# Sending TensorE's first two pipelined slots through the loop of all later slots, with idle feed-forward products in them, in place of a loop of their own

## The chip, the cores and the metric

The kernel runs on one core of one Trainium2 chip, as one launch. The metric is the device time of that core in microseconds. All engines of the core run their own instruction streams and meet only at semaphores.

## What is computed

The reference is one adaLN block over 8 sequences of 256 tokens and 128 channels. A layer norm, a modulation and an eight-head attention come first (the kernel's first part). Then the result is modulated again and goes through six layers, each a windowed attention with 16 heads and a feed-forward part:

```python
for i in range(DEPTH):                       # DEPTH = 6
    x = attn_layer(shift_tokens(x), Wqkv[i], q_scale[i], k_scale[i], Wo[i]) + x
    x = ffn_layer(shift_tokens(x), ln_g[i], ln_b[i], W1[i], b1[i], W2[i], b2[i]) + x

def ffn_layer(x, g, bln, W1, b1, W2, b2):
    mu = x.mean(-1, keepdims=True)
    var = ((x - mu) ** 2).mean(-1, keepdims=True)
    xn = (x - mu) / jnp.sqrt(var + 1e-05) * g + bln
    a, gate = jnp.split(xn @ W1 + b1, 2, -1)
    return a * jax.nn.gelu(gate, approximate=False) @ W2 + b2
```

## The kernel before

The six layers are run as a pipeline of 48 slots: slot g carries sequence g mod 8 of layer g // 8. In slot g, TensorE (`slot` of its block, L956) does

- the scores of sequence g and the end of the attention of g - 1 (`turn_q`, `turn_k`, `turn_p`, `attend`, `turn_o`, `project_out`);
- the projections of the next sequence (`q`, `k`, `v`, through `project_in`, L740);
- if `norm` is set, the two averages of the feed-forward's layer norm for f = g - 2: `mean` (L897) and `variance` (L901);
- if `ff` is set, the feed-forward products for f = g - 3 (`LAG` is 3): `gates_01`, `gate_2` and `values` (18 matmuls of 256 columns, recorded at L908 to L910) and `down` (L947, recorded at L952).

ScalarE, VectorE and GpSimd have slots of their own with the same meaning of g. SyncE moves v into place by DMA and loads the weights of the next layer. Work is ordered by hand on each engine; every wait is on a count of a semaphore. All counts start from a credit of 8 that VectorE hands out at the start, so that the first sequences wait for nothing that does not exist.

Slots 0 to 2 have no feed-forward work yet. On TensorE slot 0 is written out; slots 1 and 2 are a loop of their own (`pe.Fori(1, LAG)`, without `norm` and `ff`); behind it stand `mean(0, 5)` and `variance(0, 6)`, the layer norm of sequence 0 in banks 5 and 6 of PSUM; then comes the long loop `pe.Fori(LAG, SLOTS - 1)` over slots 3 to 46, and slot 47 is written out. In step with that piece VectorE subtracts the mean of sequence 0 at the end of its slot 2, ScalarE squares and inverts behind its slot 2 (`square`, `inverse_deviation`, `round_norm`), and GpSimd runs `divide`, `scale_norm` and `rest` behind its slot 2, where `split_up` (the low part of W1) has just run. The loops of ScalarE and GpSimd over layers begin at slot 3; VectorE's loop does too.

Of the kernel before, what the change touches and what calls it, by code (L numbers as in the profile page):

```python
# [21 lines left out]
F32 = mybir.dt.float32  # L22
# [29 lines left out]
HP = N + 1  # L52
NEG = -1e30
CREDIT = 8

LAST_BANKS = {SLOTS - 3: (2, 3, 1), SLOTS - 2: (5, 4, 0), SLOTS - 1: (2, 3, 1)}

# [9 lines left out]
def build(nc, xT, w1s, w2s, w3T, woT, cT, wmod, wqkv, scales, wo, params, w1, w2, consts, out):  # L67
    with ExitStack() as ctx:
# [210 lines left out]
        def layer_of(f):  # L279
            return f >> 3  # L280
# [12 lines left out]
        def _(sp):  # L293
# [32 lines left out]
                sp.wait_ge(s["f_prod"], CREDIT + 3 * B * layer)  # L326
                sp.dma_start(par[:, L_BA:L_END], params[layer, :, L_BA:L_END]).then_inc(s["p_h_loaded"], 16)

            def load_down(layer):
                sp.wait_ge(s["f_down"], CREDIT + B * layer)  # L330
                sp.dma_start(w2_sb[:, 0:2, :], w2[layer, 0:256, :].rearrange("(c p) e -> p c e", p=P))\
                  .then_inc(s["w_2_loaded"], 16)
                sp.dma_start(w2_sb[0:HT[2][1], 2, :], w2[layer, 256:HID, :]).then_inc(s["w_2_loaded"], 16)
                sp.wait_ge(s["f_done"], CREDIT + B * layer)
                sp.dma_start(par[:, L_B2:L_BA], params[layer, :, L_B2:L_BA]).then_inc(s["p_o_loaded"], 16)
# [56 lines left out]
            load_out(0)  # L392
            load_norm(0)
            load_hidden(0)
            load_down(0)
            sp.wait_ge(s["zeroed"], 6)
            layer_body(0, True)
            with sp.Fori(1, DEPTH - 1) as layer:
                layer_body(layer, True)
# [8 lines left out]
        def _(pool):  # L408
# [2 lines left out]
            pool.memset(w1_hi[:, :, :].bitcast(F32), 0.0).then_inc(s["zeroed"], 1)  # L411
            pool.memset(w1_lo[:, :, :].bitcast(F32), 0.0).then_inc(s["zeroed"], 1)
            pool.memset(k_t[:, :, :], 0.0).then_inc(s["zeroed"], 1)

            def low(pair, m):

# [45 lines left out]
            def divide(f):  # L462
                pool.wait_ge(s["f_rstd"], CREDIT + f + 1)
                pool.wait_ge(s["f_centred"], CREDIT + f + 1)
                pool.wait_ge(s["f_split"], CREDIT + f)
                pool.tensor_tensor(f_y, f_c, f_r, ALU.mult).then_inc(s["f_normed"], 1)

            def scale_norm(f):
                pool.wait_ge(s["f_normed"], CREDIT + f + 1)
                pool.wait_ge(s["p_n_loaded"], 16 * layer_of(f) + 16)  # L470
                pool.sem_inc(s["pool_waited"], 1)
                pool.tensor_scalar(f_y, f_y, par[:, L_G:L_G + 1], par[:, L_B:L_B + 1],
                                   ALU.mult, ALU.add).then_inc(s["f_scaled"], 1)

            def rest(f):
                pool.wait_ge(s["f_high"], CREDIT + f + 1)
                pool.tensor_tensor(f_lo[:, :], f_y, f_hi[:, :].bitcast(F32), ALU.subtract).then_inc(s["f_split"], 1)

            def slot(g, norm=True, ahead=True, more=True, after=None, layer=None):

                f = g - 2
                scale(g, 1)
                if ahead:
                    rotate(g + 1, 0, 0)
                    low(g + 1, 1)
                    rotate(g + 1, 0, 1)
                    if after == 7:
                        table(layer, 1)
                        split_weights(layer, 2)
                    scale(g + 1, 0)  # L490
                    if after == 6:
                        table(layer, 0)
                if norm:
                    divide(f)
                    scale_norm(f)
                if ahead:
                    rotate(g + 1, 1, 0)
                    if after == 6:
                        split_weights(layer, 0)
                if norm:  # L500
                    rest(f)
                if ahead:
                    if more:
                        low(g + 2, 0)
                    if after == 6:
                        split_weights(layer, 1)
                    rotate(g + 1, 1, 1)
                    if after == 2:
                        split_up(layer)
# [29 lines left out]
            rotate(0, 1, 1)  # L539
            slot(0, norm=False)  # L540
            slot(1, norm=False)
            slot(2, norm=False, after=2, layer=0)
            divide(0)
            scale_norm(0)
            rest(0)
            with pool.Fori(0, DEPTH - 1) as layer:
                first = pool.snap(layer * B)
                with pool.Fori(LAG, 6) as b:
# [17 lines left out]
        def _(pe):  # L566
# [190 lines left out]
            def k_read(n):  # L757
                pe.wait_ge(s["roped"], CREDIT + 4 * n + 4)
                pe.wait_ge(s["squared"], CREDIT + 2 * n + 2)
# [137 lines left out]
            def mean(f, bank):  # L897
                pe.wait_ge(s["f_shifted"], CREDIT + 2 * f + 2)
                pe.matmul(ps[:, bank, 0:N], mean_w, f_x, start=True, stop=True).then_inc(s["f_mean"], 1)

            def variance(f, bank):  # L901
                pe.wait_ge(s["f_squared"], CREDIT + f + 1)
                pe.matmul(ps[:, bank, 0:N], mean_w, f_sq, start=True, stop=True).then_inc(s["f_var"], 1)
# [42 lines left out]

            def down(f, bank=1, gated=f_a):  # L947
                pe.wait_ge(s["f_prod"], CREDIT + 3 * f + 3)
                pe.wait_ge(s["w_2_loaded"], 32 * layer_of(f) + 32)
                for i in range(3):  # L950
                    size = HT[i][1]
                    mm = pe.matmul(ps[:, bank, 0:N], w2_sb[0:size, i, :], gated[0:size, i, :],  # L952
                                   start=(i == 0), stop=(i == 2))
                mm.then_inc(s["f_down"], 1)
# [53 lines left out]
                        q_read(2 * g + 3)  # L1008
                        down(g - LAG)

            pe.wait_ge(s["zeroed"], 6)
            pe.wait_ge(s["bf_ready"], 2)
            q(0, 0)
            pe.wait_ge(s["ln_log"], 2 * NC)
# [3 lines left out]
            q_read(0)  # L1018
            v(0, 0)
            slot(0, att=False, norm=False, ff=False)  # L1020
            with pe.Fori(1, LAG) as g:
                slot(pe.snap(g), norm=False, ff=False)
            mean(0, 5)
            k_read(2 * LAG + 1)
            variance(0, 6)
            with pe.Fori(LAG, SLOTS - 1) as g:
                slot(pe.snap(g))
            g = SLOTS - 1
            slot(g, ahead=False)
# [35 lines left out]
        def _(act):  # L1065
# [152 lines left out]
            def square(f):  # L1218
                act.wait_ge(s["f_centred"], CREDIT + f + 1)
                act.wait_ge(s["f_var"], CREDIT + f)  # L1220
                act.activation(f_sq, f_c, ACT.Square).then_inc(s["f_squared"], 1)
# [8 lines left out]
            def round_norm(f):  # L1230
                act.wait_ge(s["f_scaled"], CREDIT + f + 1)
                act.wait_ge(s["f_value_up"], CREDIT + 2 * f)
                act.activation(f_hi[:, :], f_y, ACT.Copy).then_inc(s["f_high"], 1)
# [77 lines left out]
            ln_square(act, 2, 1)  # L1311
            ln_inverse(act, 1, 1)
            ln_square(act, 3, 1)
            act.wait_ge(s["zeroed"], 6)
            act.wait_ge(s["h0_ready"], 1)
            high(0, 0)
            high(0, 1)
# [10 lines left out]
            act.wait_ge(s["h0_ready"], B)  # L1328
            slot(0, att=False, shifted=False, norm=False, ff=False)
            slot(1, shifted=False, norm=False, ff=False)  # L1330
            slot(2, norm=False, ff=False, after=2, layer=0)
            square(0)
            inverse_deviation(0, 6)
            round_norm(0)
            with act.Fori(0, DEPTH - 1) as layer:
                first = act.snap(layer * B)
                with act.Fori(LAG, 6) as b:
# [30 lines left out]
        @block.vector  # L1368
        def _(dve):
            for name in credited:  # L1370
                dve.sem_inc(s[name], CREDIT)

            dve.memset(norm2[:, :, :], 1e-24).then_inc(s["floored"], 1)
            dve.wait_ge(s["silu_e"], 1)
# [131 lines left out]
            ln_centre(dve, 1, 1)  # L1506
            a_residual(3)
            ln_centre(dve, 2, 1)
            dve.wait_ge(s["zeroed"], 6)
            modulate(0)  # L1510
            ln_centre(dve, 3, 1)

# [82 lines left out]
                dve.scalar_tensor_tensor(of_sequence(h0, f), ps[:, bank, 0:N], par[:, L_B2:L_B2 + 1],  # L1595
                                         of_sequence(h1, f), ALU.add, ALU.add).then_inc(s["f_done"], 1)

            def slot(g, att=True, norm=True, ff=True, ahead=True, first_mean=False):
                if att:
                    normalise(g - 1, 0, 0)  # L1600
                    normalise(g - 1, 0, 1)
                centre(g, 0, 0)
                centre(g, 0, 1)
                if ahead:
                    rope_products(g + 1, 0, 0)
                    rope_products(g + 1, 0, 1)
                if ff:
                    product(g - LAG, 2, ps[:, 2, 0:N], 1)
                if norm:
                    subtract_mean(g - 2)  # L1610
                if ff:
                    product(g - LAG, 0, ps[:, 3, 0:N], 2)
                    product(g - LAG, 1, ps[:, 3, N:2 * N], 2)
                if att:
                    normalise(g - 1, 1, 0)
                if ahead:
                    norms(g + 1, 0)
                if att:
                    normalise(g - 1, 1, 1)

                centre(g, 1, 0)
                centre(g, 1, 1)
                if ahead:
                    rope_products(g + 1, 1, 0)
                    rope_products(g + 1, 1, 1)
                    if att:
                        residual(g - 1)
                    if ff:
                        add(g - LAG)
                    if first_mean:  # L1630
                        subtract_mean(0, 5)
                    norms(g + 1, 1)

            def final(b):
# [16 lines left out]
            dve.memset(h1[:, :].rearrange("p (b t) -> p b t", b=B)[:, :, 0:1], 0.0)  # L1651
            slot(0, att=False, norm=False, ff=False)
            slot(1, norm=False, ff=False)
            slot(2, norm=False, ff=False, first_mean=True)
            with dve.Fori(LAG, SLOTS - 1) as g:
                slot(dve.snap(g))
            g = SLOTS - 1
# [113 lines left out]
```

## Time and profile before

| | |
|---|---|
| three timed runs | 1684.33, 1684.33, 1689.32 us, median 1684.33 |
| profiled execution | 1680.68 us, of which the span from first to last instruction 1678.7 us |
| TensorE matmul busy | 1566.1 us (93% of the span) |
| TensorE weight loads, beside them | 1273.2 us (76%) |
| VectorE busy | 1312.9 us (78%) |
| ScalarE busy | 1279.2 us (76%) |
| GpSimd busy | 1070.6 us (64%) |
| mean granted TensorE clock | 0.974 of full speed |

A share of busy time is an average over the first part, the start of the pipeline, its long even stretch and its end, which have different limits. What a change near the start is worth is read from the stretch around it, and from whether the stretches behind it follow TensorE. In a timeline row, the number in brackets is the time that the engine sat idle just before the row, with what ended it; "issue" means that the profile shows no releaser.

### The profile page before, as it was taken

To read this page: it belongs to the slowest core of one execution; us is meant where nothing else is said; L and a number is where in the kernel's file an instruction comes from. 1 tells how busy PE (TensorE), PEld (TensorE's weight loads), DVE (VectorE), ACT (ScalarE), POOL (GpSimd) and SP (SyncE) were. 2 spreads that over 40 slices of the span, in tenths; PEclk is the share of its full clock that TensorE was granted. 3 is DMA by queue.
4 is the path that set the end of the run, shared out by engine and by line. 5 is a ranking of instruction groups with operands and counts; after the bars stand their busy time and mean duration, and the time that the engine had idled before them with its cause. 6 is when DMAs were issued, how large, how long until landed. Compare 5 with 4: busy or idle time off the path is not lost. (4 is left out here: it accounts for less than half of the span.)

```text
span 1678.7 us, 89801 instructions
## 1 busy us (share of the span) xinstructions
PE 1566.1 (93%) x36892; PEld 1273.2 (76%) x36892; DVE 1312.9 (78%) x1953; ACT 1279.2 (76%) x2006; POOL 1070.6 (64%) x783
## 2 busy tenths in 40 slices
PE   7897588999999999999999999999999999999987
PEld 3565466788887888887888887888878888888866
DVE  5576776878888888887887888878878888888853
ACT  4795456778888788887888878888778788787863
POOL 2202656678776778767769667678676787767731
PEclk9899698999999999999999999999999999999999
DMA  3000233222333223324232343222342223322221
GB/s 126 2 0 1 49 73 90 65 65 62 87 77 101 67 68 73 91 56 110 70 71 64 79 110 76 62 65 64 94 115 52 69 70 73 91 56 69 70 54 47
DMA packets 75732, 116.82 MB, mean 70 GB/s; under 512 B 17294, under 2 KB 27276, under 8 KB 74764
## 3 DMA queue, kind: packets, MB, share of 16 engines
q1 hardware_dynamic: 75660, 115.99, 27.8%
q8 instruction: 29, 0.48, 0.1%
q14 instruction: 43, 0.35, 0.1%
HBM read 19.04 MB, written 1.05 MB: 12 GB/s over the span
## 5 line engine op out<-in xcount | busy, mean ns | idle before, releaser
L430 POOL TENSOR_TENSOR arena<-arena 128x1024 f32<-128x1024 f32 x192 | 456.4, 2377 | 95.3 <-DVE arena L1526 81.5
L439 POOL TENSOR_TENSOR arena<-arena,rnorm 128x1024 f32<-128x1024 f32 x192 | 361.8, 1906 | 218.8 <-ACT rnorm L1163 218.8
L628 PE MATMUL ps<-cst,arena 64*128 64x64 f32 x6656 | 293.7, 231 | 44.7 <-issue 15.1
L628 PEld LDWEIGHTS ps<-cst,arena 64*128 64x128 f32 x6656 | 251.9, 141 | 102.9 <-issue 88.8
L1152 ACT ACTIVATE arena<-ps 128x1024 f32<-128x1024 f32 x192 | 197.1, 1026 | 112.9 <-DVE arena L1526 111.7
L1522 DVE TENSOR_TENSOR arena<-ps,rope 128x1024 f32<-128x1024 f32 x192 | 233.6, 1217 | 34.9 <-PE ps L749 34.8
L1526 DVE TENSOR_TENSOR arena<-ps,rope 128x1024 f32<-128x1024 f32 x192 | 233.1, 1214 | 0.0
L748 PE MATMUL ps<-wqkv_lo,x_hi 128*128 128x512 f32 x576 | 229.0, 397 | 0.0
L749 PE MATMUL ps<-wqkv_hi,x_hi 128*128 128x512 f32 x576 | 228.5, 397 | 0.0
L1536 DVE TENSOR_REDUCE norm<-arena 128x16 f32<-128x1024 f32 x192 | 224.4, 1209 | 0.2 <-ACT arena L1152 0.2
L745 PE MATMUL ps<-wqkv_hi,x_lo 128*128 128x512 f32 x576 | 201.2, 431 | 0.6 <-issue 0.6
L869 PE MATMUL ps<-v_sb,arena 64*32 64x66 f32 x12288 | 167.5, 228 | 12.8 <-DVE h L1595 9.0
L820 PE MATMUL ps<-k_t,arena 64*32 64x64 f32 x12288 | 170.2, 229 | 4.4 <-issue 4.4
L893 PE MATMUL ps<-arena,wo_sb 128*128 128x256 f32 x768 | 173.7, 379 | 0.0
L869 PEld LDWEIGHTS ps<-v_sb,arena 64*32 64x32 f32 x12288 | 136.9, 107 | 40.6 <-issue 33.5
L893 PEld LDWEIGHTS ps<-arena,wo_sb 128*128 128x128 f32 x768 | 145.8, 190 | 20.0
L820 PEld LDWEIGHTS ps<-k_t,arena 64*32 64x32 f32 x12288 | 137.8, 107 | 29.3 <-issue 7.5
L1548 DVE TENSOR_REDUCE rmax<-ps 128x8 f32<-128x512 f32 x192 | 130.7, 681 | 23.9 <-PE ps L820 23.8
L1552 DVE TENSOR_TENSOR arena<-ps,rmax 128x512 f32<-128x512 f32 x192 | 132.7, 691 | 14.4
L1564 DVE TENSOR_TENSOR arena<-ps,rden 128x512 f32<-128x512 f32 x192 | 132.7, 691 | 14.4
L1170 ACT ACTIVATE arena<-ps 128x1024 f32<-128x1024 f32 x96 | 98.5, 1026 | 44.9 <-PE ps L628 32.5
L1208 ACT ACTIVATE arena<-ps 128x1024 f32<-128x1024 f32 x96 | 98.5, 1026 | 41.1 <-PE ps L628 36.7
(122 smaller groups left out, 2715.8 us busy)
## 6 DMA issues: line engine op xcount, KB each, us to landing
v_sb<-v_nat SPq DMA_DIRECT2D x576, 130.0 KB
v_sb<-v_nat SPq DMA_DIRECT2D x192, 65.0 KB
wqkv_sb<-wqkv SPq DMA_DIRECT2D x6, 1536.0 KB, 6.4
v_sb<-v_sb SPq DMA_DIRECT2D x96, 65.0 KB
wo_sb<-wo SPq DMA_DIRECT2D x6, 512.0 KB, 3.9
w_sb<-w SPq DMA_DIRECT2D x6, 341.0 KB, 4.2
x<-xT SPq DMA_DIRECT2D x1, 1024.0 KB, 5.0
scl<-scales SPq DMA_DIRECT2D x6, 128.0 KB, 6.1
```

Of the source, the lines that this page charges most:

```text
L430: pool.tensor_tensor(t_cos[:, m, j, :], t_cos[:, m, j, :], t_sin[:, j, :], ALU.add)\
L439: pool.tensor_tensor(x, x, rnorm[:, H * j:H * j + H].unsqueeze(2).to_broadcast([P, H, D]), ALU.mult).then_inc(s[done], 1)
L628: mm = pe.transpose(ps[0:width, bank + t, 64 * c:64 * c + 64], src[r], ident[r, r], tile_position=(64 * t, 0))
L745: pe.matmul(ps[:, bank + c, :], x_lo[:, m, :], wqkv_hi[:, w], start=True, stop=False)
L748: pe.matmul(ps[:, bank + c, :], x_hi[:, m, :], wqkv_lo[:, w], start=False, stop=False)
L749: mm = pe.matmul(ps[:, bank + c, :], x_hi[:, m, :], wqkv_hi[:, w], start=False, stop=True)
L820: mm = pe.matmul(ps[W * w:W * w + W, bank + c, SPAN * hh:SPAN * hh + SPAN], q_t[r, 4 * g + hh, W * w:W * w + W], k_t[r, 4 * g + hh, P * m ...
L869: mm = pe.matmul(ps[W * w:W * w + W, bank + c, ON * hh:ON * hh + ON], p_t[r, h, W * w:W * w + W], v_sb[r, m, w, VD * h:VD * h + ON], start ...
L893: mm = pe.matmul(ps[:, bank, 0:N], wo_sb[:, c, :], o_t[:, c, :], start=(c == 0), stop=(c == H // 2 - 1), skip_group_check=True)
L1522: dve.tensor_tensor(t_cos[:, m, j, :].rearrange("p (h d) -> p h d", h=H), src.rearrange("p a (h d) -> p (a h) d", h=8), tc.unsqueeze(1).to ...
L1526: dve.tensor_tensor(t_sin[:, j, :].rearrange("p (h s d) -> p h s d", h=H, s=2), src.rearrange("p a (h s d) -> p (a h) s d", h=8, s=2)[:, : ...
L1536: dve.tensor_reduce(norm2[:, H * j:H * j + H, 0], sq[:, j, :].rearrange("p (h d) -> p h d", h=H), AX.X, ALU.add).then_inc(s["normed"], 1)
```

## The change

TensorE's loop over slots 1 and 2, and the mean and variance behind it, are taken out; the long loop starts at slot 1. So slots 1 and 2 now issue the feed-forward products for f = -2 and -1 and slot 1 the averages for f = -1. Nobody reads these results. The credits of the semaphores that they count up are lower by as many counts (`UNREAD`), `f_hi` and `f_lo`, which the products read, are zeroed by two more memsets on GpSimd, W2's semaphore gets a credit because its count is now compared with a number worked out from f + 8, and W2's first load no longer waits. The layer norm of sequence 0 moves into slot 2 of all four engines, where the later sequences have it.

```diff
+UNREAD = {"f_mean": 1, "f_var": 1, "f_gate_up": 4, "f_value_up": 4, "f_down": 2}
+W2_CREDIT = 32
...
-            def load_down(layer):
-                sp.wait_ge(s["f_down"], CREDIT + B * layer)
+            def load_down(layer, later=True):
+                if later:
+                    sp.wait_ge(s["f_down"], CREDIT + B * layer)
...
+            pool.memset(f_hi[:, :].bitcast(F32), 0.0).then_inc(s["zeroed"], 1)
+            pool.memset(f_lo[:, :].bitcast(F32), 0.0).then_inc(s["zeroed"], 1)
...
-            slot(2, norm=False, after=2, layer=0)
-            divide(0)
-            scale_norm(0)
-            rest(0)
+            slot(2, after=2, layer=0)
             with pool.Fori(0, DEPTH - 1) as layer:
...
             def down(f, bank=1, gated=f_a):
                 pe.wait_ge(s["f_prod"], CREDIT + 3 * f + 3)
-                pe.wait_ge(s["w_2_loaded"], 32 * layer_of(f) + 32)
+                pe.wait_ge(s["w_2_loaded"], W2_CREDIT + 32 * layer_of(f + B))
...
             slot(0, att=False, norm=False, ff=False)
-            with pe.Fori(1, LAG) as g:
-                slot(pe.snap(g), norm=False, ff=False)
-            mean(0, 5)
-            k_read(2 * LAG + 1)
-            variance(0, 6)
-            with pe.Fori(LAG, SLOTS - 1) as g:
+            pe.wait_ge(s["w_2_loaded"], W2_CREDIT + 32)
+            with pe.Fori(1, SLOTS - 1) as g:
                 slot(pe.snap(g))
...
             slot(1, shifted=False, norm=False, ff=False)
-            slot(2, norm=False, ff=False, after=2, layer=0)
-            square(0)
-            inverse_deviation(0, 6)
-            round_norm(0)
+            act.wait_ge(s["f_mean"], CREDIT)
+            slot(2, ff=False, after=2, layer=0)
             with act.Fori(0, DEPTH - 1) as layer:
...
             for name in credited:
-                dve.sem_inc(s[name], CREDIT)
+                dve.sem_inc(s[name], CREDIT - UNREAD.get(name, 0))
+            dve.sem_inc(s["w_2_loaded"], W2_CREDIT)
...
-            slot(2, norm=False, ff=False, first_mean=True)
+            slot(2, ff=False)
             with dve.Fori(LAG, SLOTS - 1) as g:
```

The waits for `zeroed` go from 6 to 8 everywhere. The rows below are built instruction rows, in the order in which an engine has them; line numbers of the changed kernel are 3 or 4 higher than before (L748 is the projection's L745, L911 to L913 are L908 to L910). TensorE before, from the end of the loop over slots 1 and 2 into the long loop:

```order
L748 MATMUL ps<-wqkv_lo,x_hi 128x512
L749 MATMUL ps<-wqkv_hi,x_hi 128x512
L1021 REGISTER_ALU
L1021 COMPARE_AND_BRANCH
L899 MATMUL ps<-f_a1,cst 128x256
L903 MATMUL ps<-f_a2,cst 128x256
L1026 UNCONDITIONAL_BRANCH
L1026 ISA
L628 MATMUL ps<-cst,arena 128x64 x16
L848 ISA
```

L899 and L903 are the mean and the variance of sequence 0, the second unconditional branch belongs to the long loop's head, and the last row is `turn_q` of slot 3. TensorE in the changed kernel, from the last projection of slot 0 into the loop:

```order
L751 MATMUL ps<-wqkv_lo,x_hi 128x512
L752 MATMUL ps<-wqkv_hi,x_hi 128x512
L1025 UNCONDITIONAL_BRANCH
L1025 ISA
L631 MATMUL ps<-cst,arena 128x64 x16
L851 ISA
L852 ISA
L757 ISA
```

The one loop is now entered right behind slot 0, and its body is that of the long loop. TensorE in the changed kernel, in the middle of the body, which slots 1 and 2 now pass too: the projection `q` and `gates_01` behind it.

```order
L748 MATMUL ps<-wqkv_hi,x_lo 128x512 x2
L751 MATMUL ps<-wqkv_lo,x_hi 128x512
L752 MATMUL ps<-wqkv_hi,x_hi 128x512
L751 MATMUL ps<-wqkv_lo,x_hi 128x512
L752 MATMUL ps<-wqkv_hi,x_hi 128x512
L922 ISA
L911 MATMUL ps<-f_hi,w1_lo 128x256
L912 MATMUL ps<-f_lo,w1_hi 128x256
L913 MATMUL ps<-f_hi,w1_hi 128x256
L911 MATMUL ps<-f_hi,w1_lo 128x256
L912 MATMUL ps<-f_lo,w1_hi 128x256
L913 MATMUL ps<-f_hi,w1_hi 128x256
```

Before, slots 1 and 2 went from these L749 rows (now L752) straight on to the projection `k`; six matmuls stand between them now, three more stand behind `k`, nine behind `v`, and three (`down`) at the end. GpSimd before, from the end of slot 2 into its loop over the layers (L459 is `split_up`, L466, L472 and L477 the layer norm of sequence 0):

```order
L420 TENSOR_TENSOR x_lo<-h0,x_hi 64x128
L423 TENSOR_TENSOR x_lo<-h0,x_hi 64x128
L430 TENSOR_TENSOR arena<-arena 128x1024
L459 TENSOR_TENSOR w1_lo<-w1_sb,w1_hi 128x2x341
L466 TENSOR_TENSOR f_a1<-f_a1 128x256
L472 ISA
L472 TENSOR_SCALAR f_a1<-f_a1,par 128x256
L477 TENSOR_TENSOR f_lo<-f_a1,f_hi 128x256
L546 UNCONDITIONAL_BRANCH
L548 UNCONDITIONAL_BRANCH
```

GpSimd in the changed kernel, the same place (L472, L478, L483 are the layer norm, L465 is `split_up`):

```order
L436 TENSOR_TENSOR arena<-arena 128x1024
L445 TENSOR_TENSOR arena<-arena,rnorm 128x1024 x2
L472 TENSOR_TENSOR f_a1<-f_a1 128x256
L478 ISA
L478 TENSOR_SCALAR f_a1<-f_a1,par 128x256
L436 TENSOR_TENSOR arena<-arena 128x1024
L483 TENSOR_TENSOR f_lo<-f_a1,f_hi 128x256
L426 TENSOR_TENSOR x_lo<-h0,x_hi 64x128
L429 TENSOR_TENSOR x_lo<-h0,x_hi 64x128
L436 TENSOR_TENSOR arena<-arena 128x1024
L465 TENSOR_TENSOR w1_lo<-w1_sb,w1_hi 128x2x341
L549 UNCONDITIONAL_BRANCH
```

The layer norm of sequence 0 has moved ahead of the last two rope sums of slot 2 and of `split_up`, which was in front of it.

## Rows read from the trace of the kernel before

**Rows 1.** The page's first line.
```profile
span 1678.7 us, 89801 instructions
```

**Rows 2.** Windows by slot: length, busy per engine (instructions), TensorE clock, DMA share, GB/s.
```profile
207.80:241.50 33.70, 27.45 (x709) 22.52 (x709) 23.72 (x32) 18.12 (x27) 18.61 (x12) 0.90 0.27 63
241.50:272.08 30.58, 26.95 (x712) 21.97 (x712) 23.73 (x33) 20.45 (x32) 19.63 (x15) 0.94 0.40 110
272.08:311.07 38.99, 32.43 (x738) 26.45 (x738) 23.07 (x34) 24.39 (x38) 22.16 (x16) 0.91 0.25 63
311.07:341.07 30.00, 29.46 (x738) 24.50 (x738) 25.05 (x36) 24.15 (x38) 20.66 (x16) 1.00 0.28 67
```

**Rows 3.** Timeline of TensorE, slots 1 and 2 and the piece behind.
```profile
207.80 1.12 PE L628 MATMUL ps<-cst,arena 64*128 64x64 f32 x16 [3.99 <-issue]
...
212.66 0.71 PE L628 MATMUL ps<-cst,arena 64*128 64x64 f32 x16 [0.76 <-issue]
...
216.34 0.43 PE L820 MATMUL ps<-k_t,arena 64*32 64x64 f32 x26 [1.03 <-issue]
216.71 0.71 PE L628 MATMUL ps<-cst,arena 64*128 64x64 f32 x16
...
223.59 0.85 PE L869 MATMUL ps<-v_sb,arena 64*32 64x66 f32 x64 [1.78 <-ACT v_nat L1185]
...
231.78 0.71 PE L628 MATMUL ps<-cst,arena 64*128 64x64 f32 x16 [1.52 <-issue]
...
241.50 0.71 PE L628 MATMUL ps<-cst,arena 64*128 64x64 f32 x16 [1.17 <-issue]
...
271.48 0.67 PE L903 MATMUL ps<-f_a,cst 128*128 128x256 f32 x2 [1.74 <-ACT f_a L1221]
```

**Rows 4.** Timeline of TensorE, slot 3 and slot 4 to the start of slot 5.
```profile
279.22 1.04 PE L628 MATMUL ps<-cst,arena 64*128 64x64 f32 x16 [3.07 <-ACT arena L1170]
...
284.35 0.71 PE L628 MATMUL ps<-cst,arena 64*128 64x64 f32 x15 [1.07 <-issue]
...
297.33 0.78 PE L820 MATMUL ps<-k_t,arena 64*32 64x64 f32 x55 [0.81 <-issue]
...
300.94 0.59 PE L628 MATMUL ps<-cst,arena 64*128 64x64 f32 x11 [1.48 <-issue]
...
309.64 1.46 PE L952 MATMUL ps<-f_a,w_sb 128*128 128x256 f32 x6
...
317.14 0.71 PE L628 MATMUL ps<-cst,arena 64*128 64x64 f32 x16
...
319.28 0.28 PE L908 MATMUL ps<-f_hi,w_lo 128*128 128x256 f32 x1
319.40 0.28 PE L909 MATMUL ps<-f_lo,w_hi 128*128 128x256 f32 x1
...
341.07 0.71 PE L628 MATMUL ps<-cst,arena 64*128 64x64 f32 x16
```

**Rows 5.** DMA queues, kind: packets, MB, share; 207.8 to 241.5, then 311 to 1600.
```profile
q8 instruction: 6, 0.10, 1.3%
...
q14 instruction: 32, 0.26, 0.1%
```

**Rows 6.** Timeline of ScalarE: end of slot 0, start of slot 3, start of slot 11.
```profile
206.67 1.03 ACT L1185 ACTIVATE v_nat<-ps 128x1024 f32<-128x1024 f32 x1
...
277.59 0.42 ACT L1233 ACTIVATE f_hi<-f_a 128x256 fp32r<-128x256 f32 x1 [4.57 <-POOL f_a L472]
...
524.65 1.02 ACT L1170 ACTIVATE arena<-ps 128x1024 f32<-128x1024 f32 x1 [3.00 <-issue]
```

**Rows 7.** Timeline of GpSimd: start, behind slot 2, and slot 11.
```profile
37.52 0.74 POOL L513 COPY f_a<-v_sb 128x256 f32<-128x256 f32 x2 [28.93 <-ACT v_sb L1097]
...
274.35 1.66 POOL L459 TENSOR_TENSOR w_lo<-w_sb,w_hi 128x682 fp32r<-128x682 f32 x1
...
525.87 1.66 POOL L459 TENSOR_TENSOR w_lo<-w_sb,w_hi 128x682 fp32r<-128x682 f32 x1
```

More of the change, by code:

```diff
@@ L394, in _ @@
             load_hidden(0)
-            load_down(0)
-            sp.wait_ge(s["zeroed"], 6)
+            load_down(0, later=False)
+            sp.wait_ge(s["zeroed"], 8)
             layer_body(0, True)
@@ L1009, in slot @@
                         down(g - LAG)
-            pe.wait_ge(s["zeroed"], 6)
+            pe.wait_ge(s["zeroed"], 8)
             pe.wait_ge(s["bf_ready"], 2)
@@ L1313, in _ @@
             ln_square(act, 3, 1)
-            act.wait_ge(s["zeroed"], 6)
+            act.wait_ge(s["zeroed"], 8)
             act.wait_ge(s["h0_ready"], 1)
@@ L1508, in _ @@
             ln_centre(dve, 2, 1)
-            dve.wait_ge(s["zeroed"], 6)
+            dve.wait_ge(s["zeroed"], 8)
             modulate(0)
@@ L1596, in add, with slot @@
                                          of_sequence(h1, f), ALU.add, ALU.add).then_inc(s["f_done"], 1)
-            def slot(g, att=True, norm=True, ff=True, ahead=True, first_mean=False):
+            def slot(g, att=True, norm=True, ff=True, ahead=True):
                 if att:
@@ L1629, in slot @@
                         add(g - LAG)
-                    if first_mean:
-                        subtract_mean(0, 5)
                     norms(g + 1, 1)
```

## Prediction

> **What bounds the kernel now.** I read the windows by slot first, because a share over the whole span [rows 1] mixes stretches with different limits. The last of these windows, slot 4, is the even stretch: 30.00 us long, of which TensorE's matmuls are busy 29.46, at full granted clock; VectorE, ScalarE and GpSimd are busy 25.05, 24.15 and 20.66 us of it [rows 2]. So TensorE sets the pace from slot 4 on, each later slot starts when TensorE has finished the one before, and the end of the run moves by what the start of slot 4 (311.07 us) moves. The change touches only what lies between 207.80 us, where TensorE begins slot 1, and that point: 33.70 + 30.58 + 38.99 = 103.27 us for three slots that at the even pace would be 90.00. The 13.3 us above that are all there is to win.
>
> TensorE's timeline says what they are. In slot 1 it stands still at three places with no releaser in sight, for 0.76, 1.03 and 1.52 us; twice this falls inside or between runs of matmuls whose inputs had long been there (the 1.03 cuts a group of 64 in two) [rows 3]. Slot 3, the first pass through the long loop, has the same kind of gap: 1.07, 0.81 and 1.48 us, again in the middle of groups [rows 4]. Slots 2 and 4, second passes of the same code, have none of these. In slot 1 the instruction queue q8 moves 6 packets of 0.10 MB together; from slot 4 to slot 44 it moves nothing [rows 5]. I read these gaps as code arriving late on the first pass of a loop body. The change has one such body in place of two.
>
> Three more waits stand in the stretch. The tail behind slot 2 is a serial piece: the variance waits 1.74 us for ScalarE's square [rows 3]. Then slot 3 waits 3.07 us for ScalarE's first copy [rows 4], because ScalarE had sat 4.57 us waiting for GpSimd's layer norm of sequence 0 [rows 6], which stood behind the 1.66 us of `split_up` [rows 7]. And slots 1 and 2 have holes for v's copy, 1.78 us in the middle of slot 1, 1.17 us at its end, where later slots have feed-forward products [rows 3] (the 1.17 has no releaser in its row, but ends just behind ScalarE's copy of v, as the 3.99 at 207.80 does).
>
> **The change, part by part.** *Entry.* Slot 1 still begins at 207.80: TensorE waits there 3.99 us [rows 3], until ScalarE has copied v out, 206.67 + 1.03 = 207.70 [rows 6]. The body's rows up to the first `turn_o` are the same as before, at the same place behind the same code, so the two gaps of 0.76 and 1.03 and the low clock after the wait (16 transposes in 1.12 us at 207.80 against 0.71 later) stay: `turn_o` at 216.71 [rows 3].
>
> *Rest of slot 1.* In slot 4 it is 341.07 - 317.14 = 23.93 us from that `turn_o` to the next slot [rows 4]. That contains all 18 feed-forward products, the average, the variance and `down`. To it come code gaps of the first pass. Slot 3 shows two in this part, 0.81 + 1.48 = 2.29 us [rows 4]; slot 1 shows one, 1.52 [rows 3]. I take 2.29, because slot 3 has this very body. The clock: over slot 3 it was 0.91, over slot 4 it was 1.00 [rows 2]; most of the loss lies behind the waits of 3.07 and 3.99 us, outside this part, so I add 0.35 us, an estimate: one group of 16 at the lower of the two levels, 1.2 against 2.4 GHz, costs 1.12 - 0.71 = 0.41 more [rows 3], and about one such group is to be expected. Sum 26.57, and slot 1 ends at 216.71 + 26.57 = 243.28. It is 35.48 us long, 1.8 more than before.
>
> *What the idle products cost.* One costs 319.40 - 319.28 = 0.12 us, 18 cost 2.2, `down` 1.46, and the average and the variance (2 passes each in 0.67, so some 0.5 each) about 1: 4.6 us a slot, already inside the even 30.00 [rows 4]. Their cover is the holes of 1.78 and 1.17 us, about 3 us a slot [rows 3]. Without any cover they would add 9.2 us in two slots; the holes hide about 5.9 of it, and the rest is paid.
>
> *Slot 2.* It is now the second pass of the body, no code gap, and its products fill the holes: 30.00 us as slot 4 [rows 2], 0.6 under the old window, which held the serial tail too. Ends at 273.28.
>
> *Slot 3.* TensorE is on its third pass: no code gap. The layer norm of sequence 0 is ahead of the end of slot 2, and nobody waits for `split_up` before ScalarE's first copy. `split_up` is late next: it starts about 5 us into slot 3 (525.87 in slot 11, after a slot whose tail is built alike), ends at about 6.8 [rows 7], and the first product that reads W1's low part comes 319.28 - 311.07 = 8.2 us into a slot [rows 4]. That cover is 1.4 us; gone, each us late is a us. 30.00 us, against 38.99 [rows 2]. Slot 4 starts at 303.28.
>
> *The small parts.* Two memsets on GpSimd fall ahead of an idle stretch of 28.93 us [rows 7]; the extra increments are a few more among many at the start; W2 is loaded there too, long before slot 1 waits for it; W1's rounding in slot 2 now waits for the unread values of the same slot, which stand well ahead of it. All nothing. Queued behind VectorE's mean subtraction, now in slot 2, are `normalise` and the norms, in the order that every later slot has.
>
> Sum: slot 1 +1.8, slot 2 -0.6, slot 3 -9.0, together -7.8 us (311.07 - 303.28 = 7.79). Against the profiled execution's own 1680.68 us (span 1678.7 [rows 1]) that is 1672.9. The median of the timed runs was 1684.33, so for a median I say 1684.3 - 7.8 = **1676.5 us**.
>
> *A rule against this.* Slot 1's three gaps come to 3.31 us and coincide with six code packets [rows 3, 5]. The Trainium skill, Runtime: NRT & Kernel Launch, Instruction fetch mechanics, says that the sequencer fetches its next block while it runs the present one and that crossing a block is mostly hidden. By that rule the gaps would not be code, and the long body would show no 2.29 us in slot 1 either; the row shows gaps in the midst of ready groups, and the sum goes by the row. Taken at its word the gaps have another cause, those of slot 3 stay in slot 3, and the gain is 7.8 - 3.4 = 4.4 us.
>
> **The bounds.** For the code gaps of the new slot 1, low 1.52 (slot 1's own), high the whole of slot 3's, with its low clock: 38.99 us for slot 1. Low gives a gain of 8.6 us, high one of 4.3.
>
> **Rivals.** *Filled but not hidden.* The products delay `k` and `v` of slot 1 by 0.7 and 1 us, VectorE and ScalarE follow, and the first pass costs all that slot 3 cost, 38.99; and slot 3 keeps its 3.07 us, because the ScalarE and GpSimd loops are entered there and load their code. Slot 4 then starts at 207.80 + 38.99 + 30.00 + 33.07 = 309.86: a gain of 1.2 us, no change. For it: ScalarE's jump back in its loop of layers does cost it 3.00 us at slot 11 [rows 6]. Against it: at slot 3 that loop is fallen into, and ScalarE's first copy there came right behind `round_norm` at 277.59 [rows 6]. With only one half of this, or if the gaps of slot 3 (1.07 + 0.81 + 1.48 = 3.36 us [rows 4]) are not code and stay there, the gain is 4.3 to 4.7.
>
> *Slower: the body no longer stays.* If the loop, at its new place in the code, were fetched anew on each jump, every pass would pay the 3.36 us of slot 3's gaps [rows 4]: 45 jumps, 151 us, some 1828 us. It decides from the third such pass on (7.8 / 3.36 = 2.3). Against it: both bodies stayed after their first pass, and the queue was silent for forty slots [rows 5]. The same page of the Trainium skill says that a taken branch to a target outside the fetched window stalls; this trace agrees for ScalarE's long loop [rows 6], not for TensorE's.
>
> *The gain is given back.* A stall at the first jumps of the other engines' loops that takes back what slot 4 wins would show as slot 11 starting less early than slot 4. Nothing but TensorE's pace lies between, so it has little chance.
>
> **How the numbers follow.** About 0.3%, 5 us, is what a measurement of this kernel tells from no change. Forecast, a gain of 5 to 9.5 us: 0.71. Filled but not hidden, a gain of 0 to 5, and given back: 0.23. Slower by a reload or by something unseen: 0.06. The range goes from 1673.0 (a gain of 11, with the bounds' 8.6 and the scatter of medians) to 1683.5 (a gain of 1, that rival): it leaves out the reload and the ends. Faster by over 0.3% 0.71, within it 0.23, slower 0.06.
>
> **What the new profile would show.** Slot 1 from 207.8 to about 243.3, with gaps of no releaser of about 0.8 and 1.0 us before 216.7 and about 2.3 us behind; six q8 packets there and none in slot 3; slots 2 and 3 at 30.0 us and clock 1.00, no 3.07 us wait for ScalarE, `split_up` ending before the gates; slot 4 near 303.3. A slot 3 of over 31 us, q8 packets in later slots, or a slot 1 over 37 us would make it wrong, and tell which step.

## The result, and the profile after

The changed kernel took 1676.92 us (median of 7 runs) against 1686.74 us for the kernel before (7 runs). The ratio is 0.9949, 95% interval 0.9933 to 0.9964, so some 8.6 us faster; it leaves out one slow run of the kernel before, of 3537.64 us. Run twice more beside the experiments the changed kernel gave 0.9960 (0.9944 to 0.9977) and 0.9943 (0.9923 to 0.9963). The forecast was 1676.5 us and a gain of 7.8.

The profiled execution of the changed kernel took 1676.92 us. From its page, the first line, the busy times and the code packets of TensorE's queue:

```profile
span 1675.1 us, 89928 instructions
...
PE 1571.2 (94%) x36944; PEld 1278.6 (76%) x36944; DVE 1313.2 (78%) x1953; ACT 1279.7 (76%) x2006; POOL 1072.1 (64%) x785
...
q8 instruction: 24, 0.39, 0.1%
```

TensorE is busier by 5.1 us (1566.1 before), with 52 more matmul records, those of the unread products and averages, while the span is shorter. The windows by slot of the changed kernel, slots 1 to 4, with the columns of [rows 2]:

```profile
208.95:244.69 35.74, 32.09 (x738) 26.50 (x738) 23.70 (x32) 18.31 (x27) 18.63 (x12) 0.90 0.25 59
244.69:273.92 29.23, 28.82 (x739) 24.20 (x738) 23.79 (x33) 20.65 (x33) 19.72 (x14) 1.00 0.39 105
273.92:303.60 29.68, 29.31 (x737) 24.39 (x737) 22.60 (x34) 24.09 (x38) 22.08 (x17) 1.00 0.35 90
303.60:333.60 30.00, 29.38 (x739) 24.44 (x738) 25.07 (x36) 24.16 (x38) 20.75 (x16) 1.00 0.28 67
```

Slots 1 to 3 together last 94.65 us, against 103.27 in [rows 2]: 8.6 us less. Slot 1 is longer by 2.0, slots 2 and 3 shorter by 1.4 and 9.3, and from slot 2 on the clock is full. The timeline of TensorE in the same execution shows where slot 1 stands still:

```profile
208.95 0.97 PE L631 MATMUL ps<-cst,arena 64*128 64x64 f32 x16 [3.86 <-issue]
...
213.61 0.71 PE L631 MATMUL ps<-cst,arena 64*128 64x64 f32 x16 [0.51 <-issue]
...
217.18 0.43 PE L823 MATMUL ps<-k_t,arena 64*32 64x64 f32 x26 [1.03 <-issue]
217.55 0.71 PE L631 MATMUL ps<-cst,arena 64*128 64x64 f32 x16
...
225.15 0.87 PE L872 MATMUL ps<-v_sb,arena 64*32 64x66 f32 x64
...
228.77 0.34 PE L872 MATMUL ps<-v_sb,arena 64*32 64x66 f32 x14 [0.44 <-issue]
...
232.64 0.42 PE L823 MATMUL ps<-k_t,arena 64*32 64x64 f32 x22 [1.67 <-issue]
...
244.69 0.71 PE L631 MATMUL ps<-cst,arena 64*128 64x64 f32 x16
```

The holes of 1.78 and 1.17 us of [rows 3] are filled. The first two gaps are where they were, one still cutting a group of 64 after 38; behind `turn_o` (217.55) there are two. Then neither slot 2 nor slot 3 has a wait of over 0.3 us: the 1.74 and the 3.07 us of [rows 3, 4] are gone. GpSimd's `split_up` in slot 3 of the changed kernel:

```profile
278.87 1.65 POOL L465 TENSOR_TENSOR w_lo<-w_sb,w_hi 128x682 fp32r<-128x682 f32 x1
```

It begins 4.95 us into the slot and ends 6.6 us in, ahead of the first product that reads it (281.84, 7.9 us in). And the queues of the changed kernel, for slot 1, then for 244.69 to 1600:

```profile
q8 instruction: 6, 0.10, 1.3%
...
q14 instruction: 35, 0.29, 0.1%
```

These are six code packets in slot 1 and, as the q14 row is the only code row of the second stretch, none on q8 from slot 2 to 1600 us.

### The profile page after: what moved, and what is told of

Read it like the earlier page. It is cut to its first block and busy times, and to the rows that moved or that the text cites. A ratio compares the mean times of both kernels' runs of the same rounds, so it can differ in the third digit from the quotient of the medians.

```text
span 1675.1 us, 89928 instructions
## 1 busy us (share of the span) xinstructions
PE 1571.2 (94%) x36944; PEld 1278.6 (76%) x36944; DVE 1313.2 (78%) x1953; ACT 1279.7 (76%) x2006; POOL 1072.1 (64%) x785
## 3 DMA queue, kind: packets, MB, share of 16 engines
HBM read 19.04 MB, written 1.05 MB: 12 GB/s over the span
## 5 line engine op out<-in xcount | busy, mean ns | idle before, releaser
L631 PE MATMUL ps<-cst,arena 64*128 64x64 f32 x6656 | 290.2, 230 | 34.4 <-issue 7.1
L1151 ACT ACTIVATE arena<-ps 128x1024 f32<-128x1024 f32 x192 | 197.0, 1026 | 113.5 <-DVE arena L1524 112.3
L752 PE MATMUL ps<-wqkv_hi,x_hi 128*128 128x512 f32 x576 | 228.6, 397 | 0.0
L748 PE MATMUL ps<-wqkv_hi,x_lo 128*128 128x512 f32 x576 | 202.1, 433 | 0.6 <-issue 0.6
L1169 ACT ACTIVATE arena<-ps 128x1024 f32<-128x1024 f32 x96 | 98.4, 1025 | 44.1 <-PE ps L631 31.9
L1184 ACT ACTIVATE v_nat<-ps 128x1024 f32<-128x1024 f32 x96 | 99.5, 1036 | 39.8 <-PE ps L752 39.8
```

The costliest lines, as they stand in the source:

```text
L631: mm = pe.transpose(ps[0:width, bank + t, 64 * c:64 * c + 64], src[r], ident[r, r], tile_position=(64 * t, 0))
L748: pe.matmul(ps[:, bank + c, :], x_lo[:, m, :], wqkv_hi[:, w], start=True, stop=False)
L752: mm = pe.matmul(ps[:, bank + c, :], x_hi[:, m, :], wqkv_hi[:, w], start=False, stop=True)
```

## The experiments

**The loop cut in two.** All else as in the changed kernel:

```diff
-            with pe.Fori(1, SLOTS - 1) as g:
-                slot(pe.snap(g))
+            for first, end in ((1, LAG), (LAG, SLOTS - 1)):
+                with pe.Fori(first, end) as g:
+                    slot(pe.snap(g))
```

> The changed kernel, with its one long TensorE loop cut in two of the same body: slots 1 and 2, then slots 3 to 46. The same work in the same order, the idle products included; only the body stands twice in the code. Theory (gaps are code that arrives late): slot 3 gets the 3.3 us of gaps that it had before, and some 0.5 to 2 us of low clock behind them, q8 moves about 6 more packets there, and the time is 3.5 to 5.5 us above the changed kernel, ratio to before 0.997 to 0.998. Rival (the gaps are not code): slot 3 stays at 29.7 us and the time is that of the changed kernel, ratio 0.995.

Measured: 1683.03 us, ratio to before 0.9994 (0.9977 to 1.0012). Windows of slots 1 to 4 of this kernel, and below them its q8 packets in slot 3:

```profile
207.68:243.30 35.62, 31.99 (x736) 26.40 (x736) 23.67 (x32) 18.29 (x27) 18.63 (x12) 0.91 0.25 59
243.30:272.55 29.25, 28.84 (x737) 24.23 (x736) 23.77 (x33) 20.65 (x33) 19.67 (x14) 1.00 0.39 105
272.55:310.54 37.99, 32.82 (x737) 26.95 (x736) 22.98 (x34) 24.17 (x38) 22.70 (x17) 0.91 0.28 72
310.54:340.50 29.96, 29.38 (x737) 24.46 (x736) 25.06 (x36) 24.10 (x38) 20.12 (x16) 1.00 0.28 67
```

```profile
q8 instruction: 6, 0.10, 1.1%
```

Slots 1 and 2 are those of the changed kernel, and slot 3, the same work in a second copy of the body, is 37.99 us against 29.68. So the rival that the gaps are not code falls. The size is more than I expected: slot 3 is 8.3 us longer in this one execution, and the expected cost was 3.5 to 5.5. The timeline of slot 3 in this kernel:

```profile
277.23 0.71 PE L631 MATMUL ps<-cst,arena 64*128 64x64 f32 x16 [1.70 <-issue]
...
281.38 0.44 PE L823 MATMUL ps<-k_t,arena 64*32 64x64 f32 x27 [1.63 <-issue]
...
294.82 0.35 PE L872 MATMUL ps<-v_sb,arena 64*32 64x66 f32 x15 [0.36 <-issue]
...
298.42 0.43 PE L823 MATMUL ps<-k_t,arena 64*32 64x64 f32 x24 [1.40 <-issue]
```

The gaps are 5.1 us, not 3.36. That the 3.07 us wait for ScalarE had given the code time to arrive in the kernel before fits this, but was not tried by itself. Of the 8.3 us, 3.5 are matmuls that take longer, at a mean clock of 0.91: TensorE is busy 32.82 us for what takes it 29.31 in the changed kernel. The other 4.8 are more idle time.

**The loop cut in three**, at slots 3 and 5, in the same way.

> The changed kernel with its long TensorE loop cut in three of the same body: slots 1 and 2, 3 and 4, 5 to 46. Theory: each further body costs the same again in its first pass, so slots 3 and 5 both have gaps of 2.3 to 3.4 us and the time is 7 to 10 us above the changed kernel, ratio to before 0.999 to 1.001, with some 12 more q8 packets. Rival (not code): ratio 0.995.

Measured: 1693.75 us, ratio 1.0057 (1.0035 to 1.0079), with 36 q8 packets on the page against 24 of the changed kernel. The first pass of the third copy, slot 5, in its windows:

```profile
340.87:379.30 38.43, 33.82 (x737) 27.50 (x736) 25.53 (x36) 24.22 (x38) 20.66 (x16) 0.87 0.23 55
```

Slot 5 costs 8.4 us more than an even slot, slot 3 in this execution 6.1. By the timed runs the second copy costs 0.34 to 0.51% (0.9994 against 0.9960, 0.9949 and 0.9943 of the changed kernel), 5.7 to 8.6 us, and the third 0.63%, 10.6 us; each of these ratios has an interval of about 0.2% to either side. I had expected 7 to 10 us for both copies together and measured some 16 to 19, by the same term as in the kernel cut in two.

**The products left out, the layer norm moved.** The changed kernel with a short loop for slots 1 and 2 that has `norm` but not `ff`; the waits that stood for the missing products are written out:

```diff
-UNREAD = {"f_mean": 1, "f_var": 1, "f_gate_up": 4, "f_value_up": 4, "f_down": 2}
+UNREAD = {"f_mean": 1, "f_var": 1}
...
-            with pe.Fori(1, SLOTS - 1) as g:
+            with pe.Fori(1, LAG) as g:
+                slot(pe.snap(g), ff=False)
+            with pe.Fori(LAG, SLOTS - 1) as g:
```

> The changed kernel, but slots 1 and 2 are again a TensorE loop of their own, without the idle feed-forward products; the mean and the variance stay inside slots 1 and 2 (sequence 0 in slot 2, an unread one in slot 1), so the serial tail behind slot 2 is gone. Theory: the tail and what followed it (the waits of 1.74 and 3.07 us and the low clock after them) are worth about 6 us of slot 3, the code of the second body costs 3.4 to 4 us, and the idle products, which are not here, cost about 2 us in slot 1 and 1 in slot 2. Slot 1 about 34, slot 2 about 28.3, slot 3 about 34 us: 96.3 us for the three against 103.3 before and 94.7 after; ratio to before 0.995 to 0.997, 1 to 2.5 us above the changed kernel and 2 to 3.5 below the kernel cut in two loops. Rival (the tail was hidden anyway and the one body is the whole gain): ratio 1.000.

Measured: 1684.14 us, ratio 1.0003 (0.9985 to 1.0021). The windows of its slots 1 to 3:

```profile
210.04:246.10 36.06, 28.83 (x714) 23.32 (x714) 23.73 (x32) 18.02 (x27) 18.58 (x12) 0.91 0.25 59
246.10:274.50 28.40, 25.50 (x712) 20.98 (x713) 23.63 (x33) 20.49 (x33) 19.55 (x14) 1.00 0.40 107
274.50:310.54 36.04, 30.27 (x736) 24.73 (x737) 22.87 (x34) 24.05 (x38) 22.21 (x17) 1.00 0.29 77
```

The three slots are 100.50 us, 4 more than expected and 2.8 less than before; the timed runs do not tell this kernel from before. The measurement agrees with the rival's number: moving the layer norm out of the serial tail gains too little to be timed, as long as a second body has to come in. In this one execution its slot 1 was 2.4 us longer than in [rows 2], with gaps of 1.05 and 1.62 us near each other.

The kernel cut in two, which has the products, took 102.86 us for the three slots, 2.4 more. These 2.4 us are not the price of the products: 1.95 of them are in slot 3, which has the same work in both kernels (37.99 us at a clock of 0.91, here 36.04 at 1.00), and slot 1 is even 0.4 us longer here. The clean comparison is slot 2, a second pass without a code gap in both: 29.25 us with the products, 28.40 without, so 0.85 us. The timed runs show no difference between the two kernels (1683.03 us with the products, 1684.14 without, on one chip).

**Where the gaps stand.** The changed kernel with 64 more instructions on TensorE before anything else:

```diff
+            for _ in range(64):
+                pe.sem_inc(s["pe_waited"], 1)
             pe.wait_ge(s["mean_loaded"], 16)
```

> The changed kernel with 64 semaphore increments more on TensorE at the very start, where it waits some 7 us for x, so that all later code stands 64 instructions further on. Theory (gaps stand where code blocks begin): every gap of slot 1 moves back by 32 matmuls (a matmul and its weight load are 2 instructions): the one that cut a group of 64 of L823 after 38 cuts one after 6, that of L872 after 50 comes after 18, that of L823 after 42 comes after 10, and the gaps of slot 47 move likewise. The time changes by what the new places cost, within 2 us either way. Rival: the gaps stay at the same matmuls.

Measured: 1678.36 us, ratio 0.9974 (0.9957 to 0.9991). Timeline of TensorE in slot 1 of this kernel:

```profile
220.40 0.80 PE L825 MATMUL ps<-k_t,arena 64*32 64x64 f32 x58 [0.70 <-issue]
...
231.86 0.70 PE L874 MATMUL ps<-v_sb,arena 64*32 64x66 f32 x46 [0.30 <-issue]
...
235.48 0.78 PE L825 MATMUL ps<-k_t,arena 64*32 64x64 f32 x54 [1.40 <-issue]
```

The rests of 58, 46 and 54 matmuls mean cuts after 6, 18 and 10 of 64, each exactly where the theory put it. The gaps hang on the place in the code, not on the matmul. The increments themselves made the first matmul late, 10.74 us against 7.01; the kernel below with the gaps at the same places and no such delay came out at 0.9952, 3.7 us better.

**The same shift at no cost.** In place of the increments, unread matmuls of 8 columns where TensorE is idle anyway:

```diff
+            for _ in range(16):
+                pe.matmul(ps[:, 0, 0:8], mean_w, mean_w[:, 0:8], start=True, stop=True)
             pe.wait_ge(s["const_loaded"], 32)
```

with 8, 16 or 24 of them there, and in two kernels 8 more ahead of the first mean. The changed kernel went along as it is.

> The changed kernel as it is, beside the three below on the same chip. Ratio to before 0.995 again, slots 1 to 3 in 94 to 95 us. If the gain seen first was luck of the chip, the ratio is within 0.3% of 1.

> The changed kernel with 8 more unread float32 matmuls of 8 columns (32 instructions, as each is two passes with a weight load each) ahead of the wait for the first scaled rows, where TensorE is idle for 4.49 us. Theory (gaps stand where code blocks begin, and what a gap costs depends on how dense the matmuls are there): the gaps of slot 1 move 16 matmuls back, so L823 is cut after 22, L872 after 34, L823 after 26. The places lie between those of the changed kernel and those of the kernel with 64 increments, and so does the time of slots 1 and 47: 0 to 4 us below the changed kernel. Rival: only the count of blocks matters, the time is that of the changed kernel.

> The same with 16 such matmuls, 64 instructions. The gaps stand where the kernel with 64 increments had them (L823 after 6, L872 after 18, L823 after 10), with slot 1 at 34.2 us and slot 47's stretch at 38.6 us against 35.7 and 41.5, but without the 4 us by which the increments made the first matmul late. Theory: 4 us below the changed kernel, ratio to before 0.992 to 0.993. Rival (the slot lengths of that one execution were chance, or the gain is given back elsewhere): ratio 0.995 like the changed kernel.

> The same with 16 such matmuls there and 8 ahead of the wait for x at the start, 96 instructions. The gaps of slot 1 move 48 matmuls back from those of the changed kernel: the first falls into the group of L816 or the end of the one before it, L872 is cut after 2, and the third falls between two groups of L823. Theory: within 3 us of the kernel with 64, either way; the one with the least gaps in slots 1 and 47 is the fastest.

Measured on one chip: the changed kernel 1677.51 us, ratio 0.9960 (0.9944 to 0.9977); with 32 instructions 1679.28, 0.9970 (0.9953 to 0.9986); with 64 1676.50, 0.9952 (0.9936 to 0.9968); with 96 1671.80, 0.9923 (0.9897 to 0.9948). Timeline of TensorE in slot 1 of the kernel with 32:

```profile
218.00 0.87 PE L825 MATMUL ps<-k_t,arena 64*32 64x64 f32 x42 [1.60 <-issue]
...
230.84 0.46 PE L874 MATMUL ps<-v_sb,arena 64*32 64x66 f32 x30 [0.32 <-issue]
...
234.78 0.76 PE L825 MATMUL ps<-k_t,arena 64*32 64x64 f32 x38 [1.86 <-issue]
```

These are cuts after 22, 34 and 26, as expected, and the kernel with 64 has its gaps after 6, 18 and 10 again. But the times did not follow my sizes: 32 gained nothing (1.8 us above the changed kernel) and 64 gained 1 us where 4 were forecast; 96 gained most. The size had been read from one execution. Slots 1 to 3 of the changed kernel itself, expected at 94 to 95 us again, were 97.30 in this second profile, because of slot 1. Below are slot 1 of that profile and slot 1 of the kernel with 96:

```profile
209.00:247.46 38.46, 33.64 (x737) 27.77 (x738) 23.98 (x32) 18.34 (x27) 18.62 (x12) 0.87 0.23 55
```

```profile
210.80:246.53 35.73, 33.75 (x736) 27.62 (x736) 23.64 (x32) 18.16 (x27) 18.63 (x12) 0.82 0.25 59
```

So slot 1 of one and the same program was 35.74 us at a clock of 0.90 and 38.46 at 0.87. The kernel with 96 is no shorter there than the changed kernel's first profile: TensorE idles less in it (2.0 us for 3.65), but its matmuls take longer (33.75 us for 32.09) at a clock of 0.82.

Because the filler might have helped by itself, the last four kernels ran together: the changed one, the one with 96 again, one with 128, and one in which the same 24 matmuls come from two loops of one matmul, so that the work is there and the shift is not:

```diff
-            for _ in range(16):
+            with pe.Fori(0, 16):
                 pe.matmul(ps[:, 0, 0:8], mean_w, mean_w[:, 0:8], start=True, stop=True)
```

> The changed kernel again, beside the three below. Ratio to before 0.995 to 0.996.

> The changed kernel with 24 unread small matmuls (96 instructions) near the start, as before. If its ratio of 0.992 stands, 0.991 to 0.994, and 4 to 7 us below the changed kernel on the same chip.

> The same 24 unread matmuls at the same places, but issued by two small loops of one matmul each, so that the same work is done while all later code is shifted by 8 matmul instructions and some of the loops instead of 96. Theory (what helps is where the code blocks begin, not the filler work): the gaps of slot 1 move by 4 to 12 matmuls from those of the changed kernel and the time is that of the changed kernel, ratio 0.995 to 0.997. Rival (the filler keeps the clock up, or the start is faster by it): ratio 0.992 as with the unrolled filler.

> The changed kernel with 32 unread small matmuls, 128 instructions, half of a block by the distance between gaps. The fill ahead of the scaled rows takes 5.4 us where 4.5 are idle, so all is 1 us late. The gaps of slot 1 stand 64 matmuls before those of the changed kernel: the first in the second `attend`'s front, the second where L823's first group ends. Theory: no more than 2 us from the kernel with 96, ratio 0.991 to 0.995.

Measured: changed 1678.32 us, 0.9943 (0.9923 to 0.9963); 96 unrolled 1671.44, 0.9908 (0.9885 to 0.9931); the same work looped 1678.18, 0.9938 (0.9917 to 0.9959); 128 1674.19, 0.9925 (0.9906 to 0.9945). The filler in loops takes the time of the changed kernel, and its gaps in slot 1 have moved by only 6 or 7 matmuls. So the shift is what gains, some 6 us (5.7 and 6.9 by the medians of the two times). With 128 the time is 2.8 us above 96, a little more than the 2 us that I had allowed. Little of the gain is in slot 1: slot 4 starts at 305.43 and 306.47 us with 96 and at 306.36 and 305.13 in the changed kernel on the same chip. Of the 4.8 and 6.7 us by which the profiled executions with 96 are shorter, 2.5 and 5.3 are at the other end of the program, in slot 47, which is written out and comes in new. Timeline of the changed kernel there, first execution, and of the kernel with 96 (second run):

```profile
1608.44 0.59 PE L631 MATMUL ps<-cst,arena 64*128 64x64 f32 x13 [1.18 <-issue]
...
1613.29 0.42 PE L823 MATMUL ps<-k_t,arena 64*32 64x64 f32 x22 [2.31 <-issue]
...
1626.79 0.80 PE L823 MATMUL ps<-k_t,arena 64*32 64x64 f32 x58 [1.46 <-issue]
...
1630.41 0.65 PE L631 MATMUL ps<-cst,arena 64*128 64x64 f32 x14 [1.59 <-issue]
...
1634.82 0.35 PE L872 MATMUL ps<-v_sb,arena 64*32 64x66 f32 x16 [2.39 <-issue]
```

```profile
1610.42 0.21 PE L827 MATMUL ps<-k_t,arena 64*32 64x64 f32 x1 [0.42 <-issue]
...
1623.08 0.64 PE L876 MATMUL ps<-v_sb,arena 64*32 64x66 f32 x37 [0.92 <-issue]
...
1627.13 0.89 PE L827 MATMUL ps<-k_t,arena 64*32 64x64 f32 x45 [1.82 <-issue]
...
1630.78 0.85 PE L876 MATMUL ps<-v_sb,arena 64*32 64x66 f32 x63 [0.58 <-issue]
```

These are 8.9 us of gaps against 3.7; in the other profiles of the same two programs they are 7.1 and 8.0 us against 4.1. From the last `down` of the loop to the first behind it, slot 47's stretch, the three executions of the changed kernel took 41.47, 38.56 and 40.29 us, the two with 96 took 36.08 and 34.99.

## Why the prediction was right, and where it was only right in sum

*Slot 1*: forecast 35.48, measured 35.74. The part to `turn_o` came out 0.3 shorter (217.55 - 208.95 = 8.60 against 8.91), the rest 27.14 against 26.57; its two gaps were 2.11 us for the 2.29 taken. That it came so near is luck in part: in two other profiles of the changed kernel slot 1 was 35.88 and 38.46 us, and the prediction had named a slot 1 of over 37 us as a sign that it was wrong.

*Slots 2 and 3*: forecast 30.00 each, measured 29.23 and 29.68. They are a little under the even slot; that ScalarE and VectorE have no gates and products in slot 2, and no `add` to wait for, is the likely reason, which no run isolates.

*The serial tail and the 3.07 us*: gone, as forecast, and `split_up` kept its cover.

*One body in place of two*: the direction was right, the size was not. The step that took the second body's price from slot 3's gaps, 3.36 us and what low clock lay beside them, was too small: the windows of the loop cut in two show 8.2 us (102.86 against 94.65), with the clock's part in it. The tail was correspondingly worth less. By kernels: before to cut in two, 103.27 to 102.86, is -0.4 us for the tail gone and the products in; then -8.2 for the one body. The timed runs say the same: the kernel cut in two is at 0.9994 of before, the one without products at 1.0003, and only the one body brings 0.9943 to 0.9960. So nearly the whole net gain is the code that need not come twice, and the rest of the change about pays for itself. How the -0.4 divides between tail and products stays open, since slot 3 of the two kernels with a second body differs by 1.95 us for the same work. The sum by slots held because slot 3 of [rows 2] contained both causes, one partly behind the other, and both went.

*What the idle products cost*: taken as 9.2 us in two slots, of which the holes hide 5.9, so some 1.7 us a slot unhidden. Slot 2 with and without them differs by 0.85 us.

*The median*: 1676.5 for 1676.92 is nearer than the working deserves. The forecast started from 1684.33 us for the kernel before, whose median was 1686.74 when both were run together. The ends of the range, 1673.0 and 1683.5, are rounded: gains of 11 and 1 us give 1673.3 and 1683.3.

*The rule that crossing a block of code is mostly hidden* (the Trainium skill, Runtime: NRT & Kernel Launch, Instruction fetch mechanics) holds for some of the crossings only. Between the gaps of slot 1 at 213.61 and 217.18 stand 126 matmuls, which with their weight loads are 252 instructions. The next crossing should be 126 matmuls on, in the group of 64 at 225.15, and that row shows no gap; ahead of it TensorE had spent 7.6 us on only 54 matmuls, 38 of them of 256 or 512 columns. The two after it fall among groups of 64 small matmuls and show, 0.44 and 1.67 us. These rows fit a rule that holds where a block is worked through slowly and fails where it is not. By it alone the second body would have cost next to nothing; it cost 6 to 8.4 us, the clock included. What the Trainium skill says there on the size of a block, 256 instructions, agrees with the 252 and the waits among them.

*The body no longer stays*: it stayed. The queue is silent from slot 2 to 1600 us, and at every shift that was tried slot 2 took 29.2 to 29.3 us.

*The end moves by what slot 4 moves*: true to within 2 to 4 us only. In the two profiled executions slot 4 begins 7.5 us earlier (slot 1 began 1.15 later) and the end comes 3.6 earlier. 1.8 us of the difference are in slot 47, 41.47 for 39.64, whose code the change has moved; some 2 are in slots 11, 19, 27 and 35, after ScalarE's jumps back: 33.03, 33.02, 32.78 and 32.69 us against 31.89, 32.92, 31.89 and 32.94. The profile of before (1680.68 us) was one of its quicker executions, which is why the two profiles differ by less than the timed runs, 8.6. Why those four slots come out at about 33 in all three profiles of the changed kernel, and two of them at 31.6 to 31.9 before and in the kernel cut in two, whose ScalarE program is that of the changed one, was not tried and stays open. Single ones of 31.6 to 31.9 are also in the kernels with 32, 64 and 96, so it is not the one long loop by itself.

## What to carry to other kernels

When gaps without a releaser show on an engine in the first pass of a loop or in written-out code, and the instruction queue moves packets there, price a copy of the body by cutting the loop in two. Idle work that lets a first, partial pass use the body of all the others can be cheaper than a second body (here 0.85 us a slot of unread products, read from slot 2, against 6 to 8 us of code). A stall that goes away may uncover another that ran behind it, so read a stretch by its whole length, and before counting on a part of it remove that part alone. Where code packets come in during the run, it is worth trying to shift where the gaps fall (some 6 us here for 96 instructions in idle time), with a control that does the same work without the shift. A size read from one profile of a first pass is not enough for that: the places of the gaps repeated exactly, their cost did not.

## What the runs showed of the hardware that I had not expected

A first pass costs more than its gaps: in slot 3 of the kernel cut in two 5.1 us of gaps brought 3.5 us more busy time for the same matmuls, the granted clock being 0.91 there and 1.00 in the passes after. The same program had slot 1 at 35.74 and 38.46 us in two executions, at clocks of 0.90 and 0.87, so one profile does not tell two placements apart. Fewer gaps can also come with a lower clock: 0.82 in slot 1 of the kernel with 96, which idled 2.0 us there and was no shorter.

Moving all code by 32 or 64 instructions changed little (0.9970 and 0.9952 against 0.9960), by 96 it gave 0.9923 and 0.9908 (against 0.9960 and 0.9943). ScalarE stands still for 2.8 to 3.3 us at each jump back in its loop of layers (3.04, 3.06, 2.83 and 2.79 in the changed kernel), and TensorE's slots there are 1.9 to 3.1 us longer than an even one in the first profiles of the two kernels.
